# Expert results written over their own rows, and two loads of expert numbers moved inside a step

## The reference

```python
h = _L0_tok_ref(x, ...)                      # patches @ W.T + b, class token, positions
h = jnp.concatenate([h, txt], axis=1)
h = h + _L0_attn_ref(_layernorm(h), ...)     # 16 heads, elu(.)+1 feature map
h = h + _L0_ffn_ref(_layernorm(h), ...)

# inside _L0_ffn_ref, for every expert e:
mask = (sel == e).astype(x.dtype)            # sel = argmax(x @ gate_w.T), rw = sigmoid(max)
xs = x * (rw * mask)[:, None]
g = xs @ w_gate[e].T
u = xs @ w_up[e].T
out = out + u * jax.nn.silu(g) @ w_down[e].T
```

## Time and profile before

| | |
|---|---|
| median of 3 runs | 491.35 us (490.98 to 492.08) |
| the profiled execution | 497.19 us, of which the span is 495.4 us |
| PE, DVE, ACT, POOL busy in the span | 447.8, 379.2, 259.9, 290.3 us |
| granted TensorE clock, mean | 0.967 |
| POOL's stores of results | 64 instructions, 62.3 us busy, 52.4 us idle just before them |

### The profile page before, as it was taken

How to read it: one execution, slowest core, us unless ns; L and a number is a source line. 1 busy time by engine, 2 the same in 40 slices (tenths; PEclk the granted TensorE clock), 3 DMA queues, 4 the chain that set the end, 5 groups by cost and what they waited for, 6 DMA issues and landing times.

```text
span 495.4 us, 12152 instructions
## 1 busy us (share of the span) xinstructions
PE 447.8 (90%) x3728; PEld 438.1 (88%) x3728; DVE 379.2 (77%) x1208; ACT 259.9 (52%) x642; POOL 290.3 (59%) x662
## 2 busy tenths in 40 slices
PE   4999999999999999999999999999679898887650
PEld 4999999999999999999999999999679888887540
DVE  5649579889988989989999988977686766556440
ACT  5344446556667766766746656665354443335100
POOL 6305224766776776776776776664564555554563
PEclk9999999999999999999999999999899998999955
DMA  8962121424231231121121121076134752111110
GB/s 286 289 211 82 56 57 58 121 70 122 63 100 47 72 93 33 34 61 39 33 61 39 37 61 46 21 194 195 40 124 147 215 187 84 67 67 58 65 67 23
DMA packets 35006, 46.13 MB, mean 93 GB/s; under 512 B 8937, under 2 KB 27100, under 8 KB 34944
## 3 DMA queue, kind: packets, MB, share of 16 engines
q1 hardware_dynamic: 25722, 30.23, 20.5%
q0 software_dynamic: 9216, 15.12, 9.9%
q10 hardware_dynamic: 6, 0.01, 0.0%
HBM read 26.61 MB, written 17.17 MB: 88 GB/s over the span
## 4 chain that ended last, share of the span: by engine, by line
PE 76%; DVE 6%; issue 6%; another core or an unknown queue 3%; POOL 3%; DMA 2%; ACT 1%; POOLq 0%; SPq 0%; DVEq 0%; ACTq 0%
PE b_w L1372 7%; PE b_w L1370 7%; PE b_att L1420 7%; PE b_w L1371 6%; PE b_kg L1370 6%; PE b_kg L1372 6%; PE b_kg L1371 6%; PE b_att L1484 5%; PE b_v L1372 3%; PE b_v L1370 3%; PE b_v L1371 3%; PE b_t L1433 2%; PE b_t L1498 2%; PE b_att L1370 2%
## 5 line engine op out<-in xcount | busy, mean ns | idle before, releaser
L720 POOL DMA_INDIRECT out<-result,rows_all x64 | 62.3, 973 | 52.4 <-DVE result L1279 31.7
L655 POOL DMA_INDIRECT sorted_rows<-rows,place x64 | 75.3, 1176 | 20.5 <-POOL place L652 10.6
L908 ACT ACTIVATE silu_g<-b_kg,rows_all 128x128 f32<-128x128 f32 x64 | 20.2, 370 | 49.6 <-PE b_kg L1372 29.8
L828 ACT ACTIVATE q_exp<-b_w,bq_s 128x228 f32<-128x228 f32 x64 | 28.9, 451 | 31.7 <-PE b_w L1372 31.7
L1370 PE MATMUL b_kg<-wkgv_hi,xnT_hi 128*114 128x264 f32 x128 | 41.9, 327 | 0.0
L616 POOL TENSOR_SCALAR ve<-mv 114x2 f32<-114x2 f32 x32 | 7.3, 228 | 58.1 <-DVE mv L1001 58.0
L1370 PE MATMUL b_w<-wo_hi,attnT_hi 128*114 128x264 f32 x124 | 41.0, 330 | 0.0
L1370 PE MATMUL b_kg<-wgu_hi,xsT_hi 128*128 x128 | 37.1, 290 | 3.2 <-DVE act_u L1289 2.2
L1370 PE MATMUL b_w<-xnT_hi,wq_hi 128*128 128x256 f32 x128 | 38.7, 302 | 1.4 <-DVE logits L1079 1.1
L1370 PE MATMUL b_v<-wkgv_hi,xnT_hi 128*114 128x256 f32 x128 | 38.8, 303 | 0.0
L811 ACT ACTIVATE den<-b_att,z_eps 114x32 f32<-114x32 f32 x32 | 9.2, 287 | 55.4 <-PE b_att L1484 52.9
(11 more groups left out here) (243 smaller groups left out, 1759.7 us busy)
## 6 DMA issues: line engine op xcount, KB each, us to landing
rows_all<-sorted_rows SPq DMA_DIRECT2D x64, 130.0 KB
rows_all<-in_x SPq DMA_DIRECT2D x18, 384.0 KB, 4.1
rows_all<-in_txt SPq DMA_DIRECT2D x32, 154.0 KB
rows_all<-in_wgu SPq DMA_DIRECT2D x8, 256.0 KB, 2.8
rows_all<-patch_out SPq DMA_DIRECT2D x48, 36.0 KB
sorted_rows<-tail_rows SPq DMA_DIRECT2D x9, 130.0 KB
rows_all<-in_wdown SPq DMA_DIRECT2D x8, 128.0 KB, 3.2
sorted_rows<-rows,place POOLq DMA_INDIRECT x64
```

What stands on the lines that cost most here:

```text
L655: G.indirect_dma_start(out=scratch[0:EXPERTS * REGION, :], out_offset=bass.IndirectOffsetOnAxis(ap=place[:, k, b:b + 1], axis=0), in_=rows ...
L720: G.indirect_dma_start(out=out, out_offset=bass.IndirectOffsetOnAxis(ap=rows_all[:, t.n, ID:ID + 1].bitcast(I32), axis=0), in_=result[:, k ...
L828: S.activation(q_exp[:, c, :], at, ACT.Exp, bias=bq_s[:, c:c + 1])
L908: last = S.activation(silu_g[:, t.slot(4)], b_gu[m.slot(2)][:, t.slot(2) * D:t.slot(2) * D + INNER], ACT.Silu, scale=rows_all[:, t.n, GAIN ...
```

## The change

DVE writes the result of a tile over the tile's own 256 values in `rows_all`, POOL stores from there, and the tensor `result` goes, with DVE's waits for stores. The mean, gain and token number of a row stand behind the 256 values and stay. Loads 2 and 3 of expert numbers move from the head of PE's step behind the gate and up products of the same step. The whole diff:

```diff
-            result = sb("result", [P, 4, D], at=room)
...
                             out=out, out_offset=bass.IndirectOffsetOnAxis(ap=rows_all[:, t.n, ID:ID + 1].bitcast(I32), axis=0),
-                            in_=result[:, k, :], in_offset=None,
+                            in_=rows_all[:, t.n, 0:D], in_offset=None,
                             bounds_check=TOKENS - 1, oob_is_err=False).then_inc(stored[k], 16)
...
                     dve.wait_ge(down_done, m.upto())
-                    if m.had(2):
-                        for t in tiles_of(m):
-                            dve.wait_ge(stored[t.slot(4)], 16 * t.rounds(4, 4))
                     for t in tiles_of(m):
                         at = t.slot(2) * D
-                        last = V.scalar_tensor_tensor(result[:, t.slot(4)], rows_all[:, t.n, 0:D], rows_all[:, t.n, MEAN:MEAN + 1],
+                        last = V.scalar_tensor_tensor(rows_all[:, t.n, 0:D], rows_all[:, t.n, 0:D], rows_all[:, t.n, MEAN:MEAN + 1],
                                                       down_bank(m)[:, at:at + D], ALU.add, ALU.add)
...
             def duo_step(j):
-                g = DUO * j.n // EXPERT_LOAD + 1
-                if j.slot(EXPERT_LOAD // DUO) == 4 and 1 < g < TILES // EXPERT_LOAD:
-                    load_experts(g)
                 if j.within(DUOS):
...
                     last.then_inc(gu_done, 1)
+                g = DUO * j.n // EXPERT_LOAD + 1
+                if j.slot(EXPERT_LOAD // DUO) == 4 and 1 < g < TILES // EXPERT_LOAD:
+                    load_experts(g)
```

## The result

| | median | lowest and highest of 12 |
|---|---|---|
| before | 492.31 us | 490.98 to 498.94 |
| changed | 497.31 us | 495.72 to 501.57 |

The ratio is 1.009, with a 95% interval of 1.006 to 1.012. I had forecast 487.8 us, and the median lies above my range. The profiled execution of the changed kernel took 496.87 us, with a span of 495.0; that of before took 497.19 with 495.4.

A forecast was written before the change was run, and what follows sets the result against it. The end of POOL's stores bounds the kernel, held back by the ring of results and the late signal. Gains of 2.3 (duos), 0.75 (last series) and 0.45 (loads) sum to 3.5 us: median 487.8 us, range 474.5 to 494.5.

The forecast's parts named there:

- the ring: Ring of results in the expert stage: DVE stands 12.1 us from 377 to 472.5 us for stores that must land.
- the late signal: Expert stage: while POOL stores back to back and PE is dense, PE's finished work becomes known only when the series ends.
- Part 1: Removing DVE's waits for stores: 26 duos take 93.1 us instead of 95.44, 2.3 us less, and 0.75 in the tail.
- the long ones' pace: Cost of a duo in POOL's series of six or eight stores before the change: 3.70 us each.
- the pause: POOL's idle 0.68 us instead of 0.30 before a long series' third duo: 0.38 us, 0.12 a duo, to go.
- the ring's two terms: Gains from removing the ring: 2.3 us over 26 duos and 0.75 us in the last series of stores.
- the late signal grows with the series: Rival for the expert stage: longer series make duos dearer; loss above 3.72 us a duo, far end 497.2 us; chance 0.20.
- middle case: The growth rival's middle: 3.80 us a duo, 98.8 us for 26 duos, 493.5 us in all.
- The last series: Final 12 stores: POOL alone limits, 11 intervals take 14.05 us instead of 14.81, 0.75 us less.
- The loads: Two loads moved behind the gate products at steps 12 and 20: gain between 0 and 1.8 us, taken as 0.45.
- The ring was the whole cause: Rival: late signals vanish with the ring, giving back 12.1 us and the tail's 0.75, 478.5 us; chance 0.18.
- Nothing moves: Rival: pauses only fill time waited anyway, leaving just the tail's 0.75 us, 490.6 us; chance 0.15.

The follow-up runs named there:

- e4: Changed kernel with results stored by plain DMAs from SyncE in sorted order and nothing on POOL in the expert stage; 456.9 us, ratio 0.9301.
- e5: Like e4, SyncE storing, but POOL makes two fills of 1,024 values for each duo; 461.22 us, ratio 0.9469.
- e9: Changed kernel with two signals of PE a step instead of four; 469.79 us against 479.24 for the kernel before, ratio 0.9795.
- e10: Kernel before, ring of results kept, with two signals of PE a step instead of four; 481.5 us against 479.24, ratio 1.0043.
- e1: Kernel before with only the ring of results taken away, the two loads left in place; 493.5 us against 489.65, ratio 1.0122.
- e3b: Changed kernel with a POOL fill of 0.98 us behind every second duo's stores; 487.82 us against 488.19, ratio 1.0015.
- e3c: Changed kernel with a POOL fill of 0.55 us behind every duo's stores; 488.09 us against 488.19, ratio 1.0008.
- e8: Changed kernel with the ring's wait put on POOL instead of DVE; 491.15 us against 488.19 for the kernel before, ratio 1.006.
- e9b: Same program as e9, run on another chip, where the kernel before took 489.66 us; median 498.2 us, ratio 1.0039.
- e17b: e9 plus two PE signals a step that nobody waits for, four sent, on the chip of e9b; 498.54 us, ratio 1.0149.
- e2: Kernel before with the ring of results kept and only the two loads moved; 488.86 us against 489.65, ratio 0.998.
- e18: e9 plus one PE signal a step that nobody waits for, three sent; 470.47 us against 479.21 for the kernel before, ratio 0.9829.
- e12: Changed kernel without high rows times low weights in gate and up products, four signals a step; 464.21 us against 479.24, ratio 0.9659.
- e13: Changed kernel without low rows times high weights in gate and up products; 492.16 us against 492.59 for the kernel before, ratio 1.001.
- e22: e12 with two more PE signals a step that nobody waits for, six sent; 464.89 us against 479.21, ratio 0.9699.

## Why the prediction was wrong

- **What bounds the kernel.** The end of POOL's stores, and behind them two causes, the ring and the late signal: right. e4 and e5 show the late signal by taking it away. The ring's own cost shows only on a prompt-signal chip, in e9 and e10; on a late-signal one, taking it away costs 1.2% (e1).
- **Part 1, the cost of a duo: the step that failed.** "If all duos go at the long ones' pace without the pause, 3.70 - 0.12 = 3.58 us". Measured: 3.80. The pauses inside the series went as foreseen, but the idle time behind a long series grew: before it was 2.73, 4.10, 2.70, 3.90 and 4.31 us, 3.55 in the mean; now behind the eight series of six it is 3.91 in the mean, and that eats the 0.38 up. A duo of those eight series costs 3.75 us, and the opening series of four, with 8.65 us for two duos, lifts the mean to 3.80. I had taken the 0.38 us out of a series and held the lateness behind it fixed, although I had just argued that the lateness hangs on the series. Breaks in POOL's stores aren't only lost time on such a chip; e3b and e3c, which put breaks in and took 3.1 to 3.3 us less than e8 beside them, show it. That the idle time behind a series grew is read from two traces of unlike executions, and that of e1 doesn't repeat it (3.06 us in the mean behind its series of six, 3.47 us a duo). What the medians show is that the kernel without the ring takes 3.9 to 5.0 us more (e1, and the change), where I had 3.1 less for the ring's two terms; how that splits over the duos of a plain execution stays open. The size in the trace was that of the rival *the late signal grows with the series*, to the digit of its middle case (3.80 us a duo, 98.8 us), to which I had given 0.20. That is luck in part: the rival's time was 493.5 us, 3.8 below the 497.31 measured, since it too was reckoned from the dear trace. The point from which it decides, 3.72, was only 0.02 above what the long series cost with the pause in; so near an edge, 0.47 for the forecast was too much.
- **Profiled against plain.** "I make no use of that difference". That was the second fault. The 5.84 us were worth reading: an execution that is so much dearer than the plain ones, in a kernel with waits of 8.83 us that vary, probably has more late signals than they have; no trace of a cheap execution of before is there to show it. Then a plain duo of before costs less than 3.67 us, and what there was to win was less. Had I put all of the difference into the 26 duos, I would have had (95.44 - 5.84) / 26 = 3.45 us for a plain duo of before, and the 93.1 us of my forecast would already have been a loss of 93.1 - 89.6 = 3.5 us. The sum by that: 491.35 + 3.5 - 1.2 = 493.7 us, slower, and still 3.6 us short of the measured time: the 3.58 us a duo of part 1 was too low as well.
- **The last series.** 14.05 us forecast and measured, 0.76 us won (0.75). Right in this trace. It holds only where the last twelve stores are one series; in other kernels without the ring they take 16.49 us (e1) and 18.43 (e9b and e17b).
- **The loads.** 0.45 us forecast, 0 to 1.8 as bounds; e2 gives 0.998 (0.9943 to 1.0016), no gain to be seen. The gap before the gate products of step 12 is gone and none has come ahead of its transposes, as foreseen; in step 20, 0.34 us stand there. That it is worth nothing fits with PE's waiting for others in most steps, but wasn't tried by itself.
- ***The ring was the whole cause*** (478.5 us, 0.18): falls on the chips of the verdict, since the ring gone makes it slower. On a prompt-signal chip something like it happens: between e10 and e9 11.7 us in the medians, 5.9 in the traces, where it gave 12.1 and 0.75. The changed kernel itself, with four signals, was not run on such a chip; e18, with three, stood at 0.9829 there.
- ***Nothing moves*** (490.6 us, 0.15): falls.
- **What could make it wrong.** "That the late signal obeys another rule than the end of a series": in part so. On the prompt-signal chips e12 and e9 have one series of 64 stores without a late signal, so a series alone doesn't hold the news in. On late-signal chips the news still comes out at about the end of a series.

Still open is what in POOL's indirect stores holds PE's signals back, and what differs between the chips. POOL being busy (e5) isn't enough, nor is the length of the series by itself (e12), and the number of signals doesn't surely matter (e9b, e17b). A lighter stream of PE isn't a cure: e13, with 20 matmuls a duo in place of 24, has late signals on a late-signal chip. Whether it helps a little can't be said, since e12 and e22, which are free of them, ran on prompt-signal chips.

## What to carry to other kernels

A wait that keeps apart what another engine issues may pay for itself: before taking it away, ask what its breaks let through, and take the lateness that hangs on a series along when the series grows. If the profiled execution is over 1% dearer than the plain ones, its variable waits are the first thing to discount. And compare two versions only on one chip and in one group of runs: e9, e12, e18 and e22 seemed to follow rules of the kernel, and all four were free of late signals only where the kernel before was fast too.

## What the runs showed of the hardware

- While GpSimd issues indirect stores one behind another (0.97 us and 0.30 between them) beside a dense PE, the news of PE's finished matmuls can reach ScalarE and VectorE 6 to 8 us late (397.04 to 403.10 us after; 461.71 to 469.39 before). PE itself then stands still for about 1 us at a time without a wait, even between transposes of one group. Plain DMAs from SyncE for the same bytes give 0.9301 of the time, and 0.9469 with GpSimd kept busy by fills.
- It depends on the chip, or on the time at which a group ran; no chip was measured twice. One kernel took 469.8 us on one and 498.2 us on another (medians of e9 and e9b), and the kernel before 479.2 and 489.7 us there. A store takes 0.97 us in both traces of e9; what differs is the idle time ahead of it, 0.52 us or up to 4.5.
- Moving two loads of 16 expert numbers into PE's registers from the head of a step to its middle gave nothing to be seen (0.998, 0.9943 to 1.0016), although the gap beside one of them was 1.04 us in the trace of before.
